# Extra full-size products on TensorE in the gate's chain and between the two merged matrices

## The chip, the cores and the metric

The kernel runs on one core of one Trainium2 chip. A core has five engines with queues of their own: TensorE (PE in the profile, its weight loads PEld), VectorE (DVE), ScalarE (ACT), GpSimd (POOL) and SyncE (SP), which issues DMAs. They run at the same time and wait for one another through semaphores. The metric is the time of one execution on the device, in microseconds. Lower is better.

## The reference

A small image-and-text transformer: 32 samples of 141 tokens (64 image patches and 77 text tokens), 128 wide. A tokenizer is followed by attention (one head), a feed-forward layer whose weights are merged for each sample, attention with eight heads, and a mixture of eight experts with two chosen for each token. The change lies in the merged feed-forward layer:

```
gh  = relu(x @ gfc1_w.T + gfc1_b)
g   = (gh @ gfc2_w.T + gfc2_b).mean(over the sample's tokens)   # 8 gate values for each sample
W1m = W1 + sum_e g[b,e] * tv_W1[e]                              # 512 x 128, one for each sample
b1m = b1 + g @ tv_b1
W2m = W2 + sum_e g[b,e] * tv_W2[e]                              # 128 x 512, one for each sample
h   = relu(x @ W1m.T + b1m)
out = h @ W2m.T + b2m
```

## The kernel before

Activations lie transposed, feature by partition: `hT` is the residual stream and `xn` the normalised one, both 128 x 4512, and each engine has its program written out by hand. `ln_pe` (L615, L621) makes a norm in twelve chunks of `CH` = 376 columns, with products of 128x128 by 128x376. PSUM is eight banks: `ps` is banks 0 and 1, `ps3a` banks 2 to 4, `ps3b` banks 5 to 7.

Around the change the work goes in four stages.

1. The gate's hidden layer: sixteen products of 282 columns (L954), ScalarE's relu (L1292), VectorE's sums over the tokens (L1527) into `ghm`.
2. The gate's chain, in which each step waits for the last: TensorE multiplies `ghm` by `gfc2` (L956), VectorE sets `g9` (L1531, L1533), TensorE spreads it over the partitions (L958), VectorE makes `gcol` and `gblk` (L1535, L1537). Between, TensorE makes the merged biases with five products of 32 columns (L961), which VectorE copies out (L1540).
3. The merge: the rows of both matrices come as products with `gblk`. Of each row of the matrices the base and its eight task vectors are nine inputs, three rows go into one product, so a product has 27 active rows and 96 columns (three rows by 32 samples). Four products stand in the array at once, in its four groups of 32 rows, and write four banks (L969). Twenty products are a set, with one load of 320 KB (`tvc`, five buffers deep, issued by SyncE at L499 when the set five before it is done). There are `SETS` = 18 sets, the last with four products only; `W1_SETS` = 9 of them make the first matrix. Sets alternate between banks 0 to 3 and banks 4 to 7; ScalarE copies two banks of a set into `arena` (L1298) and VectorE the other two (L1545). TensorE begins set s when set s-2 has been copied out.
4. The feed-forward layer: for each of 32 samples four products with the first matrix (L991), relu on ScalarE and VectorE (L1313, L1314, L1555), four products with the second (L1001). The merged weights of a sample are first gathered from `arena` into `wst`, the first matrix by ScalarE (L1308; for samples 0 and 1 by GpSimd, L687, as soon as nine sets are done), the second by GpSimd (L693). These loops wait for all 18 sets.

Of the kernel before, what the change touches and what calls it, by code (L numbers as in the profile page):

```python
# [33 lines left out]
CH = 376  # L34
# [33 lines left out]
W1_SETS = -(-F // (20 * NJ))  # L68
# [52 lines left out]
def reuse(eng, sem, u, depth):  # L121

    if is_known(u):
        if u >= depth:
            eng.wait_ge(sem, u - depth + 1)
    else:
        eng.wait_ge(sem, u - depth + 1)
# [84 lines left out]
def early_fusion(nc, patches, text, noise, vectors, turned, spread, tok, attn0, ffn, attn1, moe, mrows, const, out):  # L212
# [3 lines left out]
    with ExitStack() as ctx:  # L216
        def sb(name, shape, dt=F32, scope=None):
            return (scope or ctx).enter_context(nc.sbuf_tensor(name, shape, dt))
# [8 lines left out]
        def S(name):  # L227
            if name not in sems:
                sems[name] = ctx.enter_context(nc.semaphore(name))
            return sems[name]  # L230
# [5 lines left out]
        bank = [ps[0][:, :], ps[1][:, :]] + [ps3a[:, i, :] for i in range(3)] + [ps3b[:, i, :] for i in range(3)]  # L236

        hT = sb("hT", [P, T])
        xn = sb("xn", [P, T])
# [9 lines left out]
        def C(name, rows=P):  # L249
            a, n = CONST[name]  # L250
            return cst[0:rows, a:a + n]
# [4 lines left out]
        def W(name):  # L256
            return wT[:, SLOT[name], :]
# [145 lines left out]
        def chunk(buf, c, n=CH):  # L403
            return buf[:, bass.ds(c * n, n)]
# [21 lines left out]
        def normed(eng, name, chunks):  # L426

            eng.wait_ge(S("ln_out"), NCH * NORMS.index(name) + chunks)
# [236 lines left out]
        def _(pool):  # L665
# [97 lines left out]
            def scatter(g, i):  # L763
                src, _, rows = rows_of(g, i)
                if i == SPLIT[g] + g:
                    pool.wait_ge(S("xs_clear"), 16)
                    pool.wait_ge(S("x2_set"), SPLIT[g + 1] + g + 1)
                    pool.wait_ge(S("aux_set"), g + 1)
                for k, buf in enumerate((src, xr2[0:rows, i])):
                    pool.indirect_dma_start(xs[:, :], bass.IndirectOffsetOnAxis(ap=m_at[0:rows, k, i:i + 1], axis=0),  # L770
                                            buf, None, oob_is_err=True).then_inc(S("scattered"), 16)
# [39 lines left out]
        def _(pe):  # L811
# [138 lines left out]
            for t in range(B // 2):  # L950
                if t < 4:
                    normed(pe, "ln2", 9 + t)
                reuse(pe, S("gh_done"), t, 4)
                pe.matmul(bank[t % 4][:, 0:GB], W("gfc1"), chunk(xn, t, GB), start=True, stop=True).then_inc(S("gh_mm"), 1)  # L954
            pe.wait_ge(S("gh_sum"), B // 2)
            pe.matmul(bank[4][0:E, 0:B], W("gfc2")[:, 0:E], ghm[:, :], start=True, stop=True).then_inc(S("g_mm"), 1)  # L956
            pe.wait_ge(S("g9_ready"), 2)
            pe.matmul(bank[5][:, 0:B], C("rep", E + 1), g9[:, 0:B], start=True, stop=True).then_inc(S("grep_mm"), 1)  # L958
            pe.wait_ge(S("tvb_in"), 64)
            for k in range(5):  # L960
                mm = pe.matmul(bank[6][:, k * B:(k + 1) * B], tvb[:, k * P:(k + 1) * P], g9[:, 0:B], start=True, stop=True, skip_group_check=True)  # L961
            mm.then_inc(S("bm_mm"), 1)
            pe.wait_ge(S("gblk_ready"), 1)

            def merge(n, r, h):
                pe.wait_ge(S(f"tv_in{r}"), n * 16 + 16)
                for c in range(min(5, NM - 5 * (5 * n + r))):
                    for i in range(4):
                        mm = pe.matmul(bank[4 * h + i][:, c * NJ * B:(c + 1) * NJ * B], tvc[32 * i:32 * i + KM, r, c * P:(c + 1) * P],  # L969
                                       gblk[32 * i:32 * i + KM, :], start=True, stop=True, skip_group_check=True)  # L970
                mm.then_inc(S("mg_mm"), 1)
            for s in range(SETS):
                if s == 1:
                    pe.wait_ge(S("bm_copied"), 1)
                if s >= 2:
                    pe.wait_ge(S("mg_act"), s - 1)
                    pe.wait_ge(S("mg_dve"), s - 1)
                merge(s // 5, s % 5, s % 2)
            pe.wait_ge(S("mg_act"), SETS)
            pe.wait_ge(S("mg_dve"), SETS)  # L980
# [1075 lines left out]
```

## Time and profile before

| | us |
|---|---|
| runs shown (3) | 745.31, 745.4, 747.85; median 745.4 |
| profiled execution, its own time | 745.01 |
| its span | 743.2 |
| PE busy | 638.4 (86%) |
| DVE / ACT / POOL busy | 501.8 / 443.5 / 307.6 |
| granted TensorE clock, mean over the span | 0.911 |

The span is what the profiler records of the program; the execution's own time is 1.8 us more. The granted clock is a share of 2.4 GHz: 1.00 is 2.4 GHz and 0.50 is 1.2 GHz. In a timeline a row is a run of like instructions: start, length, engine, line, operation, tiles (out<-in), count, and in brackets the idle time before it with what ended it. "128x480 f32" is partitions by elements.

### The profile page before, as it was taken

Reading aid. Unit: us, or ns where it says so; the run is one execution under the profiler, and the core shown is the slowest. Engines: PE = TensorE matmul, PEld = TensorE weight load, DVE = VectorE, ACT = ScalarE, POOL = GpSimd, SP = SyncE. Lnnn points to the kernel's source line nnn. Section 1 sums busy time; section 2 is a strip of 40 time slices with the busy share of each in tenths; the row PEclk is TensorE's granted clock in tenths of the full one; section 3 lists DMA queues with packets and bytes.
Section 4 is the critical chain, followed back from the end, with each engine's and each line's share of the span. In section 5 each row is a group of like instructions: output and inputs, shape, how many; then the busy total and the mean of one; then the engine's idle time right before and its main releaser. Section 6 shows DMA issues by size and latency. Waiting matters only on the chain.

```text
span 743.2 us, 17507 instructions
## 1 busy us (share of the span) xinstructions
PE 638.4 (86%) x5635; PEld 541.0 (73%) x5635; DVE 501.8 (68%) x1399; ACT 443.5 (60%) x1185; POOL 307.6 (41%) x502
## 2 busy tenths in 40 slices
PE   5698999899999998999989988946889999999800
PEld 2247986699999656888878877835879888888700
DVE  4446784655455564888898895866787787878614
ACT  4386455744888697777767764603646566656500
POOL 0200000001555301222354686589772376777642
PEclk9999999955999998999999997977899999999955
DMA  8911323053000499940000000000142778888547
GB/s 257 280 52 65 120 96 105 1 144 90 1 0 0 164 353 360 334 136 2 2 3 2 31 27 20 23 32 19 48 128 58 250 274 273 283 276 282 188 145 265
DMA packets 65639, 96.39 MB, mean 130 GB/s; under 512 B 6279, under 2 KB 48868, under 8 KB 65573
## 3 DMA queue, kind: packets, MB, share of 16 engines
q1 hardware_dynamic: 56004, 82.64, 34.6%
q0 software_dynamic: 5344, 10.80, 4.1%
q10 hardware_dynamic: 4224, 2.10, 0.9%
q8 instruction: 38, 0.62, 0.3%
q14 instruction: 29, 0.23, 0.1%
HBM read 51.25 MB, written 44.26 MB: 129 GB/s over the span
## 4 chain that ended last, share of the span: by engine, by line
PE 46%; POOL 15%; DVE 12%; ACT 11%; issue 9%; DMA 5%; SPq 1%; POOLq 0%; DVEq 0%; ACTq 0%
POOL rows_by_token L800 9%; PE ps L1062 3%; DMA rows_by_token<-yrow,homei 3%; PE ps3b L1102 3%; POOL rows_by_expert L770 3%; PE ps L969 2%; PE ps L991 2%; PE ps3a L991 2%; PE ps3b L1001 2%; PE ps3a L1089 2%; PE ps3a L1001 2%; DVE h_f L1891 2%; ACT wst L646 2%; PE ps3b L969 1%; PE ps L817 1%
## 5 line engine op out<-in xcount | busy, mean ns | idle before, releaser
L800 POOL DMA_INDIRECT rows_by_token<-yrow,homei x93 | 94.4, 1015 | 57.6 <-DVE yrow L1909 30.9
L1395 ACT CAST h_hi<-h_f 128x384 fp32r<-128x384 f32 x86 | 44.1, 513 | 76.6 <-DVE h_f L1891 69.6
L1345 ACT ACTIVATE arena<-ps3a,arena 128x141 f32<-128x141 f32 x192 | 55.7, 389 | 7.8 <-DVE arena L1775 7.1
L1914 DVE TENSOR_TENSOR h_lo<-h_f,h_hi 128x384 fp32r<-128x384 f32 x86 | 47.8, 556 | 17.6 <-ACT h_hi L1395 16.7
L693 POOL COPY wst<-arena 128x512 f32 (+1 forms) x32 | 36.0, 1127 | 41.1 <-DVE arena L1545 15.3
L1751 DVE RECIPROCAL arena<-ps 128x141 f32<-128x141 f32 x32 | 33.3, 1042 | 23.0 <-PE ps L1065 23.0
L1327 ACT ACTIVATE arena<-ps,vec,cst 128x141 f32<-128x141 f32 x32 | 15.1, 471 | 48.8 <-PE ps L1080 47.9
L1775 DVE TENSOR_REDUCE arena<-ps3a 128x2 f32<-128x282 f32 x96 | 38.6, 443 | 6.4 <-PE ps3a L1089 6.3
L770 POOL DMA_INDIRECT rows_by_expert<-xr,m_at x36 | 35.7, 992 | 11.0 <-issue 11.0
L770 POOL DMA_INDIRECT rows_by_expert<-xn,m_at x32 | 34.2, 1070 | 8.3 <-issue 8.3
L969 PE MATMUL ps3a<-gblk,tvc 27*128 27x96 f32 x262 | 36.2, 413 | 0.0
L969 PEld LDWEIGHTS ps3a<-gblk,tvc 27*128 27x128 f32 x262 | 35.1, 311 | 0.0
L734 POOL COPY arena<-arena 128x104 f32<-128x104 f32 x32 | 8.7, 272 | 63.6 <-ACT arena L1347 63.6
L1102 PE MATMUL ps3b<-cst,arena 128*128 128x128 f32 x256 | 34.7, 280 | 0.0
L1308 ACT COPY wst<-arena 128x512 f32 (+1 forms) x30 | 34.2, 1140 | 0.0
L726 POOL TENSOR_TENSOR arena<-arena,cst 128x104 f32<-128x104 f32 x32 | 11.9, 372 | 50.4 <-ACT arena L1329 50.1
L1891 DVE TENSOR_TENSOR h_f<-ps,h_s 128x384 f32<-128x384 f32 x43 | 23.9, 556 | 12.8 <-ACT h_s L1392 6.4
L1102 PEld LDWEIGHTS ps3b<-cst,arena 128*128 128x128 f32 x256 | 30.6, 146 | 0.0
L687 POOL COPY wst<-arena 128x512 f32<-128x512 f32 x2 | 2.0, 1061 | 67.0 <-DVE arena L1545 67.0
L1124 PE MATMUL ps3a<-h_hi,wb 128*128 128x384 f32 x62 | 26.2, 423 | 4.0 <-issue 2.1
L682 POOL COPY arena<-xn 128x52 f32<-128x52 f32 x8 | 1.8, 232 | 61.5 <-PE ps3b L916 42.4
L1089 PE MATMUL ps3a<-arena 32*128 32x141 f32 x384 | 26.4, 310 | 0.1
(405 smaller groups left out, 2324.7 us busy)
## 6 DMA issues: line engine op xcount, KB each, us to landing
rows_by_expert<-zeros SPq DMA_DIRECT2D x1, 18915.0 KB, 61.1
wb<-expert_parts SPq DMA_DIRECT2D x31, 512.0 KB, 4.0
wb<-expert_parts SPq DMA_DIRECT2D x31, 256.0 KB
expert_parts<-arena SPq DMA_DIRECT2D x18, 384.0 KB, 2.8
xrow<-rows_by_expert SPq DMA_DIRECT2D x31, 195.0 KB
tvc<-merge_rows SPq DMA_DIRECT2D x18, 320.0 KB, 3.0
rows_by_token<-zeros SPq DMA_DIRECT2D x2, 2304.0 KB, 44.9
ysum<-rows_by_token SPq DMA_DIRECT2D x10, 320.0 KB, 6.0
```

What stands on the lines that cost most here:

```text
L693: pool.tensor_copy(wst[:, r, F:2 * F], merged_for(1, t)).then_inc(S("f_w2"), 1)
L770: pool.indirect_dma_start(xs[:, :], bass.IndirectOffsetOnAxis(ap=m_at[0:rows, k, i:i + 1], axis=0), buf, None, oob_is_err=True).then_inc(S ...
L800: pool.indirect_dma_start(yt[:, :], bass.IndirectOffsetOnAxis(ap=homei[:, q, s:s + 1], axis=0), yrow[:, q, s, :], None, oob_is_err=True).t ...
L969: mm = pe.matmul(bank[4 * h + i][:, c * NJ * B:(c + 1) * NJ * B], tvc[32 * i:32 * i + KM, r, c * P:(c + 1) * P], gblk[32 * i:32 * i + KM, ...
L1089: mm = pe.matmul(bank[2 + i][:, e * N:e * N + N], b_q[rows, q, e, 0:P], b_k[rows, q, :], start=True, stop=True, skip_group_check=True)
L1102: mm = pe.transpose(bank[6 + h // 4][:, (h % 4) * P:(h % 4) * P + P], b_e[:, r, h, 0:P], ident)
L1308: act.copy(wst[:, r, 0:F], merged_for(0, t)).then_inc(S("f_w1"), 1)
L1345: ins = act.activation(b_e[:, q, h, :], bank[2 + i][:, (h % 2) * N:(h % 2) * N + N], ACT.Exp, bias=b_nm[:, q, h:h + 1])
L1395: act.copy(h_hi[:, s, 0:n], h_f[:, s, 0:n]).then_inc(S("h_hi"), 1)
L1775: dve.tensor_reduce(b_nm[:, q, 2 * i:2 * i + n], bank[2 + i][:, 0:n * N].rearrange("p (h n) -> p h n", h=n), AX, ALU.max, negate=True).the ...
L1891: dve.tensor_tensor(h_f[:, s, :], bank[UB_[k]][:, 0:M], h_s[:, s, :], ALU.mult).then_inc(S("prod"), 1)
L1914: dve.tensor_tensor(h_lo[:, s, :], h_f[:, s, :], h_hi[:, s, :].bitcast(F32), ALU.subtract).then_inc(S("h_lo"), 1)
```

## The change

The change adds nine products of 128x128 by 128x376 that nothing reads, of the constant matrix `centre` with a chunk of `xn`. Two stand behind the gate's hidden layer, one behind the product with `gfc2`, and one behind the five bias products, all into bank 7 (`keep_running`). Five stand between set 8 and set 9 of the merge, behind set 9's waits, into bank 4, which set 9 then overwrites. No other instruction and no wait changes.

```
+            def keep_running(n):
+                pe.matmul(bank[7][:, 0:n], C("centre"), chunk(xn, 0, n), start=True, stop=True, skip_group_check=True)
+            for k in range(2):
+                keep_running(CH)
             pe.wait_ge(S("gh_sum"), B // 2)
             pe.matmul(bank[4][0:E, 0:B], W("gfc2")[:, 0:E], ghm[:, :], start=True, stop=True).then_inc(S("g_mm"), 1)
+            keep_running(CH)
             pe.wait_ge(S("g9_ready"), 2)
             pe.matmul(bank[5][:, 0:B], C("rep", E + 1), g9[:, 0:B], start=True, stop=True).then_inc(S("grep_mm"), 1)
             pe.wait_ge(S("tvb_in"), 64)
             for k in range(5):
                 mm = pe.matmul(bank[6][:, k * B:(k + 1) * B], tvb[:, k * P:(k + 1) * P], g9[:, 0:B], start=True, stop=True, skip_group_check=True)
             mm.then_inc(S("bm_mm"), 1)
+            keep_running(CH)
             pe.wait_ge(S("gblk_ready"), 1)
...
                 if s >= 2:
                     pe.wait_ge(S("mg_act"), s - 1)
                     pe.wait_ge(S("mg_dve"), s - 1)
+                if s == W1_SETS:
+                    for k in range(5):
+                        pe.matmul(bank[4 * (s % 2)][:, 0:CH], C("centre"), chunk(xn, k, CH), start=True, stop=True, skip_group_check=True)
                 merge(s // 5, s % 5, s % 2)
```

TensorE's row in the program between the gate's hidden layer and the first set, before (`ghm`, `g` and `gblk` are the gate's tiles, `tvb` the bias rows, `tvc` a set's load):

```order
L954 MATMUL ps3a<-xn,wT 128x282 x2
L956 MATMUL ps3a<-ghm,wT 8x32
L958 MATMUL ps3b<-g,cst 128x32
L961 MATMUL ps3b<-g,tvb 128x32 x5
L969 MATMUL ps<-gblk,tvc 128x96 x2
```

The same place in the changed kernel:

```order
L954 MATMUL ps3a<-xn,wT 128x282 x2
L957 MATMUL ps3b<-xn,cst 128x376 x2
L961 MATMUL ps3a<-ghm,wT 8x32
L957 MATMUL ps3b<-xn,cst 128x376
L964 MATMUL ps3b<-g,cst 128x32
L967 MATMUL ps3b<-g,tvb 128x32 x5
L957 MATMUL ps3b<-xn,cst 128x376
L976 MATMUL ps<-gblk,tvc 128x96 x2
```

The four new products are the rows of L957; the fourth stands between the bias products and set 0.

TensorE's row where set 8 (banks 0 to 3) ends and set 9 (banks 4 to 7) begins, before:

```order
L969 MATMUL ps<-gblk,tvc 128x96 x2
L969 MATMUL ps3a<-gblk,tvc 128x96 x3
L969 MATMUL ps3b<-gblk,tvc 128x96 x3
L969 MATMUL ps3a<-gblk,tvc 128x96
L969 MATMUL ps3b<-gblk,tvc 128x96 x3
```

And in the changed kernel:

```order
L976 MATMUL ps<-gblk,tvc 128x96 x2
L976 MATMUL ps3a<-gblk,tvc 128x96 x2
L987 MATMUL ps3a<-xn,cst 128x376 x5
L976 MATMUL ps3a<-gblk,tvc 128x96
L976 MATMUL ps3b<-gblk,tvc 128x96 x3
L976 MATMUL ps3a<-gblk,tvc 128x96
```

The three products "ps3a x3" of before were the last two of set 8 and the first of set 9; the five new ones now stand between them.

## Rows read from the trace of the kernel before

**Rows 1.** The page: busy time, and TensorE's granted clock in 40 slices of 18.6 us.
```profile
PE 638.4 (86%) x5635; PEld 541.0 (73%) x5635; DVE 501.8 (68%) x1399; ACT 443.5 (60%) x1185; POOL 307.6 (41%) x502
PEclk9999999955999998999999997977899999999955
```

**Rows 2.** Stretch, length; busy and count of PE, PEld, DVE, ACT, POOL; PEclk; DMA.
```profile
140.50:143.90 3.40, 3.38 (x15) 2.35 (x13) 3.19 (x8) 3.40 (x8) 0.00 (x0) 1.00 0.00 0
143.90:147.30 3.40, 1.81 (x28) 1.68 (x29) 1.73 (x8) 0.51 (x2) 0.00 (x0) 1.00 0.00 0
147.40:183.40 36.00, 36.00 (x681) 36.00 (x675) 19.89 (x33) 16.32 (x32) 2.05 (x2) 0.50 0.43 121
183.40:185.10 1.70, 0.45 (x6) 0.21 (x1) 1.55 (x4) 1.31 (x4) 0.00 (x0) 0.50 0.00 0
185.10:188.20 3.10, 3.04 (x13) 3.07 (x14) 0.63 (x2) 0.70 (x3) 2.05 (x2) 0.50 0.00 0
```

**Rows 3.** Timeline of PE, from the gate's hidden layer to the first sets.
```profile
142.77 1.11 PE L954 MATMUL ps3a<-xn,wT 128*128 128x282 f32 x4
144.95 0.23 PE L956 MATMUL ps3a<-ghm,wT 128*8 128x32 f32 x2 [1.07 <-DVE ghm L1527]
145.72 0.40 PE L958 MATMUL ps3b<-g,cst 9*128 9x32 f32 x2 [0.55 <-DVE g L1533]
...
146.87 0.35 PE L969 MATMUL ps3a<-gblk,tvc 27*128 27x96 f32 x2
...
147.06 0.28 PE L969 MATMUL ps3a<-gblk,tvc 27*128 27x96 f32 x2
...
147.17 0.28 PE L969 MATMUL ps3a<-gblk,tvc 27*128 27x96 f32 x2
```

**Rows 4.** Timeline of PE where set 1 ends and set 2 begins, and of DVE.
```profile
150.91 0.42 PE L969 MATMUL ps<-gblk,tvc 27*128 27x96 f32 x1
...
151.13 0.42 PE L969 MATMUL ps<-gblk,tvc 27*128 27x96 f32 x1
...
151.51 1.22 DVE L1545 COPY arena<-ps3b 128x480 f32<-128x480 f32 x2 [0.81 <-PE ps3b L969]
153.64 1.22 DVE L1545 COPY arena<-ps3a 128x480 f32<-128x480 f32 x2 [0.91 <-PE ps3a L969]
```

**Rows 5.** Timeline of PE in the norm before the gate.
```profile
124.83 0.80 PE L621 MATMUL ps3b<-wst,cst 128*128 128x376 f32 x2
125.47 0.80 PE L615 MATMUL ps<-hT,cst 128*128 128x376 f32 x2
```

**Rows 6.** DMA issues of 140 to 200 us, and the rate in 40 slices of 1.5 us.
```profile
GB/s 0 0 0 0 0 0 11 217 97 154 199 167 90 179 213 71 180 208 123 141 178 212 65 184 205 13 0 0 0 0 0 0 0 11 0 0 0 0 0 0
tvc<-merge_rows SPq DMA_DIRECT2D x13, 320.0 KB, 3.0
```

**Rows 7.** Timeline where the feed-forward layer begins.
```profile
185.16 2.22 PE L991 MATMUL ps<-xn,wst 128*128 128x141 f32 x8 [1.31 <-ACT arena L1298]
185.19 2.05 POOL L693 COPY wst<-arena 128x512 f32<-128x512 f32 x2 [15.35 <-DVE arena L1545]
...
188.69 1.13 PE L1001 MATMUL ps3a<-hbuf,wst 128*128 128x141 f32 x8
...
189.65 1.12 PE L991 MATMUL ps<-xn,wst 128*128 128x141 f32 x8
189.85 0.37 DVE L1560 SCALAR_TENSOR_TENSOR xn<-ps3a,bmb,xn 128x141 f32<-128x141 f32 x1 [0.33 <-PE ps3a L1001]
```

**Rows 8.** Busy time of stretches elsewhere, columns as in rows 2.
```profile
399.90:403.30 3.40, 2.06 (x26) 1.64 (x25) 3.30 (x14) 1.64 (x6) 0.96 (x4) 1.00 0.00 0
...
287.30:290.60 3.30, 2.94 (x23) 2.26 (x22) 1.97 (x6) 3.30 (x14) 1.09 (x4) 1.00 1.06 361
```

**Rows 9.** TensorE's products by line in 399.9 to 403.3, then in 287.3 to 290.6.
```profile
L1089 PE MATMUL ps3a<-arena 32*128 32x141 f32 x12 | 0.8, 304 | 0.0
...
L1089 PE MATMUL ps3a<-arena 32*128 32x141 f32 x12 | 2.0, 319 | 0.1
```

More of the change, by code:

```diff
@@ L954, in _, with keep_running @@
                 pe.matmul(bank[t % 4][:, 0:GB], W("gfc1"), chunk(xn, t, GB), start=True, stop=True).then_inc(S("gh_mm"), 1)
+            def keep_running(n):
+                pe.matmul(bank[7][:, 0:n], C("centre"), chunk(xn, 0, n), start=True, stop=True, skip_group_check=True)
+            for k in range(2):
+                keep_running(CH)
             pe.wait_ge(S("gh_sum"), B // 2)
             pe.matmul(bank[4][0:E, 0:B], W("gfc2")[:, 0:E], ghm[:, :], start=True, stop=True).then_inc(S("g_mm"), 1)
+            keep_running(CH)
             pe.wait_ge(S("g9_ready"), 2)
@@ L962, in _ @@
             mm.then_inc(S("bm_mm"), 1)
+            keep_running(CH)
             pe.wait_ge(S("gblk_ready"), 1)
@@ L977, in _ @@
                     pe.wait_ge(S("mg_dve"), s - 1)
+                if s == W1_SETS:
+                    for k in range(5):
+                        pe.matmul(bank[4 * (s % 2)][:, 0:CH], C("centre"), chunk(xn, k, CH), start=True, stop=True, skip_group_check=True)
                 merge(s // 5, s % 5, s % 2)
```

## The prediction
> **What bounds the kernel now.** I read the page first: TensorE is busy for 86% of the span, and the strip of its granted clock, which is 9 nearly everywhere, has two slices of 5 at 149 to 186 us, the ninth and tenth of the strip [rows 1]. So the next view was busy time by stretch around there [rows 2]. The reader is to see three things. In the gate's chain, 143.9 to 147.3 us, TensorE was busy for 1.81 of 3.40 us, with thin products, and still had clock 1.00. In the merge, 147.4 to 183.4, it was busy for 36.00 of 36.00 us at 0.50, which is 1.2 GHz, while VectorE worked 19.89 and ScalarE 16.32 us: TensorE alone bounds this stage, at half its speed. The clock came back only after 3 us of full-size feed-forward products (185.1 to 188.2).
>
> Then the timelines, for what a set of the merge costs. Groups of four L969 products follow one another every 0.11 us before the clock fell (146.87, 147.06, 147.17, the first pair with a bias product between) [rows 3] and every 0.22 us after (150.91, 151.13) [rows 4]. A set of 20 products is ten such steps: 2.13 us, as VectorE's copies of it are apart (151.51, 153.64), and 1.07 us at clock 1.00. VectorE's two copies of a set take 1.22 us, and it waited 0.91 us before each.
>
> **The change part by part.** A product of 376 columns takes 0.63 us in a stream at clock 1.00 (124.83, 125.47) [rows 5]; at 0.50 no row shows one, and I estimate twice that, 1.26 us, as the merge's steps double.
>
> First and second new product. The gate layer's last four records start at 142.77 and stream 0.24 us each (0.63 x 282/376 / 2), to 143.71; two products more end at 144.97. The product with `gfc2` started at 144.95, after 1.07 us of waiting for VectorE's sums [rows 3]. Cost 0 to 0.05 us; the cover is that wait.
>
> Third: from about 145.05 to 145.68, where TensorE waited for `g9` until 145.72 [rows 3]. Cost 0 to 0.05 us.
>
> Fourth: it stands behind the bias products, and the merge followed on them with no gap (146.87 and 147.06 are sets' products already). Nothing hides it: 0.65 us. What is queued behind it is set 0, for which ScalarE and VectorE wait. For all four I take +0.7 us; bounds 0.6 and 1.0.
>
> What they buy, if it comes: the low-work stretch at clock 1.00 after which the clock fell now holds 1.9 to 2.5 us of full-size products in 3.4 us, against none. I expect the clock to stay at 1.00 there. No row shows this chain with them.
>
> The merge at clock 1.00. TensorE then needs 1.07 us for a set, less than VectorE's 1.22, so what is late next is the handing back of banks. Set s+2 starts when set s has been copied out: product time 1.07, from the set's end to VectorE's first copy 0.38, copies 1.22, back to TensorE 0.08. The 0.38 is an estimate: at half clock it was 0.60 (150.91 to 151.51) [rows 4], and in the feed-forward layer at clock 1.00 VectorE began 0.20 us after the set of products ended (189.65 to 189.85) [rows 7]; it lies between. A cycle of two sets is 2.75 us, a set 1.38. From set 0's start, set 9 would start at 4 x 2.75 + 1.25 = 12.25 us.
>
> The five products before set 9. They stand behind its waits, so they begin when it could have begun: +3.13 us (5 x 0.63) for set 9 and all odd sets behind it; VectorE copies set 8 in the meantime and then waits. Set 17 starts at 26.4 and set 16 at 24.9; set 16 is copied out at 27.6, set 17 (a fifth of a set) 0.4 us later, and the feed-forward layer starts at 28.1. Before, it was 185.16 - 146.86 = 38.3 [rows 3, 7]. Gain 10.2 us.
>
> Bounds on the set's time. Below: VectorE alone, 1.22 us, which gives another 2.6 us. Above: the loads. 13 of the 18 sets' loads go during the merge, 320 KB each; the highest rate of a slice was 217 GB/s [rows 6], which is 1.51 us for a set and costs 13 x 0.13 = 1.7 us. They land in 3.0 us [rows 6] and are issued four sets, 5.5 us, ahead, so I take them as hidden. If a load of every set were late by all that the clock gains, the gain would be 0.
>
> The feed-forward start. L991's first start to L1001's first took 3.53 us at clock 0.50; in the steady part such a pair of steps is 1.92 (two of 188.69 to 189.65) [rows 7]. GpSimd's first copy of two (2.05 us from the start) ends within it. Gain 1.6 us; bounds 0 and 1.8. It is 0 where the clock falls at the merge's end, where TensorE has about 1.5 us without work and a short set before it, as now (0.45 busy of 1.70 us) [rows 2]: I give that 4 in 10, at 1.6 us.
>
> GpSimd's copies of the first matrix for samples 0 and 1 move earlier with set 8; nothing waits for them. All that follows is a chain without a fixed time in it, so it moves as a whole. But the later falls of the clock (slices of 7 and 8) [rows 1] need not repeat as they were: one of them, shown as an 8 in an 18.6 us slice, is worth some 2 us either way.
>
> Sum: +0.7 - 10.2 - 1.6 = -11.1 us against the profiled execution's 745.0, so 733.9; the median of the runs is 0.4 above that execution, so 734.3. With part of the risk at the merge's end, 734.5.
>
> One rule of the Trainium skill ("TensorE: Matmul & The Clock Gate", LDWEIGHTS) speaks against this sum: it gives a weight load as its columns over 1.2, in ns, at whatever clock, and a set is bound by its loads. By it a set would take 2.13 us still. The steps of 0.11 us at clock 1.00 [rows 3] are against it. The same page (What's actually happening) says that activity releases the throttle; with TensorE busy for all of 36.00 us at 0.50 [rows 2] the trace does not agree for 27-row products, and if it did the change would have nothing to win beyond the first microseconds.
>
> **The rivals.** The question is whether the merge, which did not raise the clock in 36 us, holds it. For: it stayed at 1.00 in stretches with fewer products and real gaps, as at 399.9 to 403.3 (busy 2.06 of 3.40 us, with 32-row products among them). Against: it fell after 287.3 to 290.6, where TensorE was busy for 2.94 of 3.30 us, most of it with 32-row products [rows 8, 9]. Raising and holding need not ask the same of the engine, and the merge at full rate leaves gaps of only a fifth.
>
> A. It falls in both halves (the slower side). Per us at clock 1.00 the merge gains (2.13 - 1.38) / 1.38 = 0.55 us. Against it stand 0.7 us and the five products, which at half clock until it rises (about 3.1 us, as at the feed-forward start) cost 3.1 + 2.5 x 0.63 = 4.7 us. So the change loses if the merge has less than 10 us at clock 1.00 in all. With 2 us in each half: 745.4 + 5.4 - 2.2 = 748.6; with none 750.8.
>
> B. It falls in the first half only, after some 3 us, and the five products bring it back for good: 0.7 + 4.7 - 1.7 (3 x 0.55) - 8 sets x 0.75 - 1.6 = -3.9, 741.5.
>
> C. The loads bound the sets at up to 1.51 us: 736.
>
> D. A set is no faster at clock 1.00: 0.7 + 3.13 - 1.6 = +2.2, 747.6. Only the rule of the skill speaks for it; the measured steps against.
>
> **How the numbers follow.** Forecast 0.66; A 0.14; B 0.13; C 0.04; D 0.03. The forecast's own range is 730.5 to 738: below by VectorE's bound and a later fall that is gone, above by the fall at the feed-forward start and a later one more. With C and most of B the range is 730 to 743. A measurement of this kernel tells about 0.5%, 3.7 us. Faster than 741.7: 0.66 + 0.04 + 0.6 of B = 0.78. Within: the rest of B, D, and the part of A with some full clock, 0.17. Slower: 0.05.
>
> **What would show it.** Clock 1.00 from 144 us on through the merge; VectorE's pairs of copies 1.3 to 1.4 us apart, with one hole of about 3 us more before set 9's; set 0 some 0.7 us after its old time; the first L991 at about 175.6 and the first L1001 1.9 us behind it; the span about 11 us shorter and the stages behind 190 us unchanged. I am wrong if the clock is 0.50 in the merge (A, B), if pairs are over 1.5 us apart with TensorE waiting for `tvc` (C), or if the steps of L969 stay at 0.21 us at clock 1.00 (D).

## The result and the profile after

The changed kernel takes 732.97 us (median of four, 732.7 to 733.94) against 746.09 before (745.31 to 747.85): ratio 0.9846, 95% interval 0.9815 to 0.9878. Timed again on another chip it was 733.3 against 743.14, ratio 0.9878 (0.9832 to 0.9924). The forecast was 734.5 in a range of 730 to 743. The ratios leave out executions that lie more than 1.5% above the fastest of their kernel, and they are not the quotients of the medians beside them.

Single executions of one kernel lie several us apart (before: 735.5 to 749.5 in one group of eleven), and their mean clock differs with them (0.926 in the first, 0.909 in the last). In the two profiles of the changed kernel, and of the kernel with three products (e3, e6), the clock's falls stand at different places. So below the profiles are compared stage by stage, and totals only as medians.

Busy time by stretch of the changed kernel, columns as in [rows 2]: the chain, sets 0 to 8, the five products, sets 9 to 16, the end of the merge, the feed-forward start.

```profile
143.90:147.30 3.40, 3.40 (x20) 2.23 (x19) 1.42 (x7) 0.01 (x1) 0.00 (x0) 1.00 0.00 0
147.70:159.80 12.10, 10.97 (x350) 10.30 (x352) 9.23 (x16) 8.16 (x16) 0.00 (x0) 1.00 0.63 177
159.90:163.00 3.10, 3.10 (x25) 2.00 (x21) 1.30 (x3) 1.02 (x2) 1.27 (x2) 1.00 0.81 253
163.00:173.20 10.20, 9.42 (x290) 8.48 (x290) 7.06 (x12) 6.12 (x12) 0.80 (x1) 1.00 0.47 138
...
174.80:178.00 3.20, 2.22 (x19) 2.08 (x19) 1.45 (x5) 1.22 (x6) 1.89 (x2) 0.82 0.00 0
```

The chain has no empty stretch left, and the clock is 1.00 through the merge, where before it was 0.50 from 0.5 us behind its start on. It falls just behind the merge, in the first feed-forward products (0.82 over 174.8 to 178).

The timeline of TensorE through the chain, which answers to [rows 3]. L957 is the new line, L976 the merge.

```profile
142.26 1.11 PE L954 MATMUL ps3a<-xn,wT 128*128 128x282 f32 x4
143.21 1.42 PE L957 MATMUL ps3b<-xn,cst 128*128 128x376 f32 x4
144.57 0.22 PE L961 MATMUL ps3a<-ghm,wT 128*8 128x32 f32 x2
144.72 0.90 PE L957 MATMUL ps3b<-xn,cst 128*128 128x376 f32 x2
145.55 0.40 PE L964 MATMUL ps3b<-g,cst 9*128 9x32 f32 x2
145.80 1.28 PE L967 MATMUL ps3b<-g,tvb 9*128 9x32 f32 x10
147.00 0.90 PE L957 MATMUL ps3b<-xn,cst 128*128 128x376 f32 x2
147.83 0.35 PE L976 MATMUL ps<-gblk,tvc 27*128 27x96 f32 x2
```

The last gate products started 0.51 us earlier in this execution than in that of before, so set 0, at 147.83 against 146.86, is 1.48 us late. The first two products cost 0.13 us (L961 at 144.57 against 144.95 less 0.51), the third 0.21 more (L964), and the fourth the rest, 1.1.

The copies by VectorE, which answer to [rows 4]:

```profile
157.62 1.22 DVE L1555 COPY arena<-ps3a 128x480 f32<-128x480 f32 x2 [0.40 <-PE ps3a L976]
158.76 1.21 DVE L1555 COPY arena<-ps3b 128x480 f32<-128x480 f32 x2
160.37 1.22 DVE L1555 COPY arena<-ps3a 128x480 f32<-128x480 f32 x2 [0.40 <-PE ps3a L976]
165.04 1.22 DVE L1555 COPY arena<-ps3b 128x480 f32<-128x480 f32 x2 [3.44 <-PE ps3b L976]
166.18 1.21 DVE L1555 COPY arena<-ps3a 128x480 f32<-128x480 f32 x2
```

The copies of every second set are 2.75 us apart (157.62, 160.37), where it was 2 x 2.13. Set 9's come at 165.04 in place of 161.51 (158.76 + 2.75): the five products cost 3.53 us at that place. Set 10's follow on them at once, at 166.18, in place of 163.12 (160.37 + 2.75), so the even sets behind the five are 3.06 us late and not 3.53.

The start of the feed-forward layer, which answers to [rows 7]. L1001 is L991 of before, L1011 is L1001.

```profile
174.81 0.28 PE L976 MATMUL ps3b<-gblk,tvc 27*128 27x96 f32 x3
176.08 1.51 PE L1001 MATMUL ps<-xn,wst 128*128 128x141 f32 x8 [0.98 <-ACT arena L1308]
177.38 2.09 PE L1001 MATMUL ps3a<-xn,wst 128*128 128x141 f32 x8
179.26 1.61 PE L1011 MATMUL ps3a<-hbuf,wst 128*128 128x141 f32 x8
```

TensorE had no work for about 1 us after the short last set, the clock fell some way into the first products, and L1011 starts 3.18 us behind L1001 (3.53 before, 1.92 forecast without a fall).

By stage, in us, the profiled executions of all kernels. "Chain" is from the gate layer's first product (L954) to the merge's first, "merge" from there to the first feed-forward product, "start" from there to the first product with the second matrix, "sum" from the gate layer's first product to the last of the feed-forward layer.

| kernel | chain | merge | start | sum | fall in the merge |
|---|---|---|---|---|---|
| before | 11.71 | 38.30 | 3.52 | 113.44 | at its start |
| changed | 13.18 | 28.24 | 3.18 | 105.00 | no (at its end) |
| changed, again | 13.19 | 28.39 | 2.12 | 103.68 | no |
| e1: four, no five | 13.19 | 26.34 | 2.12 | 101.63 | no |
| e2: five only | 11.75 | 37.62 | 3.59 | 112.87 | at its start, back at the five |
| e3: first three | 12.05 | 25.88 | 2.12 | 100.03 | no |
| e4: four of 32 rows | 12.19 | 39.12 | 3.89 | 115.62 | at its start |
| e6: first three, again | 12.05 | 25.63 | 2.12 | 99.78 | no |
| e7: three and one at the end | 12.05 | 26.01 | 2.12 | 100.16 | no |
| e8: first two | 11.83 | 38.02 | 3.80 | 113.57 | at its start |
| e9: third only | 12.20 | 38.71 | 3.89 | 115.30 | at its start |
| e10: four, short fourth | 12.77 | 31.07 | 3.89 | 108.33 | half way |
| e11: three and one before set 9 | 12.05 | 25.91 | 2.12 | 100.06 | no |
| e12: three and two before set 9 | 12.05 | 27.34 | 3.57 | 102.97 | no (at its end) |

Only the changed kernel and the kernel with three products were profiled twice; each other row is one execution.

Of the 11.1 us by which the changed kernel's profiled span is shorter, 8.4 lie in these stages, 0.5 ahead of them and 2.1 to 2.2 behind, where the clock's falls came at other places. The strip of the clock after has no 5 at 149 to 186 us any more, against [rows 1]:

```profile
PEclk9999999999999997999999999976899999999955
```

### The profile page after: what moved, and what is told of

It is laid out like the page before. It is cut to its first block, busy times and chain, and to the rows that moved or that the text cites. A ratio compares the mean times of both kernels' runs of the same rounds, so it can differ in the third digit from the quotient of the medians.

```text
span 732.1 us, 17543 instructions
## 1 busy us (share of the span) xinstructions
PE 624.2 (85%) x5653; PEld 524.9 (72%) x5653; DVE 503.4 (69%) x1399; ACT 443.7 (61%) x1185; POOL 304.8 (42%) x502
## 4 chain that ended last, share of the span: by engine, by line
PE 61%; DVE 11%; ACT 10%; POOL 7%; issue 5%; DMA 4%; SPq 1%; POOLq 0%; DVEq 0%; ACTq 0%
PE ps3a L1134 4%; PE ps L1072 3%; PE ps3b L1112 3%; PE ps3a L1136 3%; PE ps3a L1135 3%; POOL rows_by_expert L770 3%; PE ps3a L1099 2%; PE ps3a L1001 2%; PE ps L1001 2%; PE ps3a L1011 2%; PE ps3b L1011 2%; DMA wb<-expert_parts 2%; PE ps L1134 2%; PE ps L1136 2%; PE ps L1135 2%
## 5 line engine op out<-in xcount | busy, mean ns | idle before, releaser
L743 POOL TENSOR_SCALAR xn<-hT,m_mv,m_rs 128x128 f32<-128x128 f32 x32 | 25.8, 805 | 0.3 <-ACT m_rs L1371 0.2
L1099 PE MATMUL ps3b<-arena 32*128 32x141 f32 x128 | 24.9, 315 | 0.0
```

Source lines behind the costliest of these rows:

```text
L1099: mm = pe.matmul(bank[2 + i][:, e * N:e * N + N], b_q[rows, q, e, 0:P], b_k[rows, q, :], start=True, stop=True, skip_group_check=True)
```

## The experiments

All are the changed kernel with an edit. "Held" means clock 1.00 through the merge.

**e1, the chain's four products without the five.**

```
-                if s == W1_SETS:
-                    for k in range(5):
-                        pe.matmul(bank[4 * (s % 2)][:, 0:CH], C("centre"), chunk(xn, k, CH), ...)
```

> The four products of the chain without the five before set 9. Theory 1 (the chain's products keep the clock at 1.00 and the merge holds it; the five are a cost): set 9's copies come 3.5 us earlier than in the changed kernel, clock 1.00 through the merge, 733.0 - 3.5 = 729.5 us. Theory 2 (the five are needed to hold the clock in the second half): it falls in the second matrix's sets, which then take 2.13 instead of 1.38 us; about 3 us slower than the changed kernel, 736.

Median 735.05 us (728.84 to 739.59, four runs) against 742.59 before; ratio 0.9889 (0.9801 to 0.9978). In the profile the merge held, in both halves:

```profile
147.90:160.20 12.30, 11.17 (x362) 10.63 (x364) 9.40 (x16) 8.16 (x16) 0.00 (x0) 1.00 0.64 183
160.30:174.20 13.90, 11.60 (x332) 10.47 (x327) 11.14 (x20) 9.47 (x20) 2.07 (x2) 1.00 0.51 150
```

So the five are not what holds it in that execution. But the merge is only 1.9 to 2.1 us shorter than in the two profiles of the changed kernel, not 3.5, and the median is no lower than the changed kernel's 733 (with 733.0 - 3.5 = 729.5 expected). Two things are in the merge's part of this. The five had cost the even sets 3.06 us and not 3.5. And in set 10 VectorE waited 1.53 us where it had waited 0.40, and TensorE stood still ahead of it with nobody to wait for:

```profile
161.57 1.21 DVE L1552 COPY arena<-ps3b 128x480 f32<-128x480 f32 x2
164.32 1.22 DVE L1552 COPY arena<-ps3a 128x480 f32<-128x480 f32 x2 [1.53 <-PE ps3a L976]
```
```profile
162.48 0.42 PE L976 MATMUL ps<-gblk,tvc 27*128 27x96 f32 x4
163.60 0.35 PE L976 MATMUL ps3a<-gblk,tvc 27*128 27x96 f32 x2 [0.70 <-issue]
```

This is a stop of 0.70 us with the releaser "issue", within set 10. The changed kernel's merge has no such stop of the matmuls; whether the five covered it isn't shown, since e3 and e6 below have no five either and no long stop. One run of the four had a mean clock of 0.93 and 739.59 us; e10 shows one fall that may stand behind that, if not the only one.

**e2, the five without the chain's four.**

```
-            for k in range(2):
-                keep_running(CH)
...
-            keep_running(CH)      # the third
...
-            keep_running(CH)      # the fourth
```

> The five products before set 9 without the four of the chain. Theory 1: the clock falls in the chain as before, nine sets go at 2.13 us, the five start at 1.2 GHz and bring the clock back, costing about 4.7 us; eight sets then gain 0.75 us each and the start of the feed-forward layer up to 1.6: 746.1 + 4.7 - 6.0 - 1.6 = 743 us, 745 if the clock falls again at the merge's end. Theory 2 (the five give most of the gain): 736 or less.

Ratio 0.9961 (0.9913 to 1.0008); median 742.03 against 742.59, ten runs from 732.01 to 748.94. The stretches, sets 0 to 8, the five, sets 9 to 17, feed-forward start:

```profile
147.40:167.30 19.90, 19.90 (x352) 19.44 (x349) 10.77 (x19) 9.03 (x18) 0.00 (x0) 0.50 0.48 135
167.40:170.80 3.40, 3.40 (x7) 1.76 (x7) 0.26 (x1) 0.05 (x1) 2.02 (x2) 0.58 0.35 96
170.90:183.80 12.90, 11.15 (x331) 9.91 (x329) 9.57 (x18) 8.45 (x18) 0.00 (x0) 1.00 0.36 105
184.10:187.60 3.50, 3.50 (x16) 3.50 (x17) 0.64 (x2) 1.20 (x3) 2.02 (x2) 0.54 0.00 0
```

Theory 1 holds in the totals and in this profile: the chain's products make the gain. The clock rose while the five ran, and the second half then kept it, but they began at 166.28 and set 9 at 171.59, 5.31 us, which eats most of what the eight sets gain; the clock fell again at the end. One run, 732.01 us with a mean clock of 0.942, is as fast as the changed kernel; it has no profile, so whether its merge held is open.

**e3, the first three products of the chain.** The fourth and the five are out.

```
             mm.then_inc(S("bm_mm"), 1)
-            keep_running(CH)
```

> Only the first three products of the chain: the fourth, behind the bias products, and the five are out. Theory 1: the first three stand in waits that TensorE has anyway and are enough; the fourth cost 1.1 us of its own. Clock 1.00 through the merge, 729.5 - 1.1 = 728.4 us. Theory 3 (the bias products and the merge's first set have too little work in them without the fourth): the clock falls at the merge's start, 746 us or a little more.

Median 729.93 us (725.48 to 734.41), ratio 0.9806 (0.9737 to 0.9876). The merge held, and set 0 came 1.14 us earlier than with four (12.05 against 13.19).

```profile
150.10:175.90 25.80, 22.23 (x692) 20.82 (x691) 20.81 (x37) 17.64 (x36) 2.09 (x2) 1.00 0.58 169
```

The fourth isn't needed, and theory 3 falls for three products. The profiled run is the slowest (734.41 us, mean clock 0.935); it had falls of the clock at 57 and 64 us, far ahead of the change, so a low mean clock alone doesn't tell that the merge fell.

TensorE stood still for less at the place of e1's stop, with no product before set 9:

```profile
165.01 0.27 PE L975 MATMUL ps3a<-gblk,tvc 27*128 27x96 f32 x1
165.43 0.24 PE L975 MATMUL ps3a<-gblk,tvc 27*128 27x96 f32 x1
```

From start to start that is 0.42 us in place of a step of 0.11; in e1 it was 0.97, and in the second profile of this kernel (e6) no such gap stands there. The merge is 0.5 to 0.7 us shorter than e1's (25.88 and 25.63 against 26.34).

**e4, four products with 32 active rows.** Their length is the same, but a quarter of the array's rows is used.

```
-                pe.matmul(bank[7][:, 0:n], C("centre"), chunk(xn, 0, n), ...)
+                pe.matmul(bank[7][:, 0:n], C("centre")[96:P, :], chunk(xn, 0, n)[96:P, :], ...)
```

> As the first kernel of these (four products in the chain, no five), but the four have 32 active rows of 128, the same 128 output rows and 376 columns and so the same length. Theory 1 (full-size work holds the clock; thin products, as the merge's, count for little): the clock falls at the merge's start as before, and the products are only a cost, 746.1 + 1.5 = 747.6 us. Theory 4 (any products that fill the gaps hold it): clock 1.00 in the merge, 729.5 us.

Median 743.83 against 742.59, ratio 1.0021 (0.9985 to 1.0057). The chain was as full of products as ever (first row), and the clock fell all the same:

```profile
141.00:145.90 4.90, 4.90 (x26) 3.11 (x24) 3.44 (x10) 2.33 (x5) 0.00 (x0) 1.00 0.00 0
146.30:183.70 37.40, 37.40 (x693) 37.40 (x691) 19.99 (x33) 16.31 (x32) 2.07 (x2) 0.50 0.41 117
```

Theory 4 falls. Filling the gaps doesn't do it: products of 128 rows did, those of 32 didn't (nothing between was tried). The total is 3.8 us under the 747.6 that was expected, of which 3.5 is that the kernel before ran at 742.59 here and not at 746.1; against it e4 is 1.2 us slower, where 1.5 was expected. The chain is only 0.5 us longer than before (12.19), so thin products between thin ones delay less than full-size ones; the rest of the 2.2 us by which its sum is longer comes behind, where the clock was down already at the first set (from 145.9 us on).

**The changed kernel again (e5), three products again (e6), three and one at the merge's end (e7), two products (e8)**, in one group on one chip.

> The changed kernel once more, on the chip and beside the kernels of this group, since single runs of one kernel spread over some us. Theory 1: from the gate layer's first product to the feed-forward layer's last 105.0 us, or 103.4 where the clock does not fall at the merge's end; 8.4 to 10 less than before; total 9 to 13 us below before.

> The first three products of the chain alone, again, beside the changed kernel. Theory 1: 3 to 5 us less than the changed kernel of this group (the five cost 3.5 in place, the fourth 1.1), 100 us from the gate layer's first product to the feed-forward layer's last. Rival: the total is the same within 1 us because the falls of the clock behind the merge come back and even it out.

> The first three products, and one more between set 16 and set 17 of the merge, where TensorE waits for the copies anyway. Theory 5 (the clock falls at the start of the feed-forward layer in part of the runs, for lack of work at the merge's end, at some 1.7 us): 0.5 us less than the three alone on average and no run with a fall there; the product itself costs at most 0.3 us. Rival: no fall there without it either, so it only costs, up to 0.3 us.

> Only the first two products of the chain. Behind them stand the product with gfc2, 0.5 us of waiting, the spreading product and the bias products, all thin. Theory 1: two full-size products in the stretch after which the clock fell are enough in most runs, 100 us from gate layer to feed-forward end; total as with three. Theory 3: the 2 us of thin work and waiting behind them let it fall at the merge's start, 113 us and the total of before.

```
# e7: three products, and in the loop over the sets
+                if s == SETS - 1:
+                    pe.matmul(bank[4][:, 0:CH], C("centre"), chunk(xn, 0, CH), ...)
# e8: as e3, without the third product as well
```

| | median | runs | ratio to before (743.14) |
|---|---|---|---|
| e5, changed | 733.3 | 728.89 to 734.57 | 0.9878 (0.9832 to 0.9924) |
| e6, three | 728.9 | 727.67 to 734.81 | 0.9846 (0.9794 to 0.9898) |
| e7, three and end | 732.41 | 731.09 to 738.49 | 0.9883 (0.9831 to 0.9935) |
| e8, two | 734.36 | 728.55 to 738.01 | 0.9869 (0.9805 to 0.9933) |

The changed kernel's stages (e5) took 103.68 us here, near the 103.4 of theory 1 without a fall at the end. In place, three products are 3.9 us shorter than four and the five (99.78 against 103.68); the medians say 4.4, but the intervals of the ratios overlap. In e6 four runs lie at 727.67 to 729.01 with a mean clock of 0.946 and more, and two at 733.51 and 734.81 with 0.936 and less.

e7 isn't settled. Its profile has no fall at the feed-forward start and nor has that of e6; the medians don't show a gain, and in place the extra product costs at most 0.4 us (100.16 against 99.78, and 100.03 in e3).

e8 suggests that two are on the edge. In the profiled run the chain had full-size work only at its start (first row), and the clock fell for the whole merge; another run, 728.55 us with a mean clock of 0.947, is like those of kernels whose merge held; it wasn't profiled.

```profile
142.40:145.70 3.30, 2.75 (x36) 2.09 (x38) 1.53 (x7) 0.06 (x1) 0.00 (x0) 1.00 0.00 0
146.00:181.30 35.30, 35.30 (x668) 35.30 (x665) 19.55 (x32) 16.32 (x32) 2.05 (x2) 0.50 0.44 123
```

**e9, the third product alone, and e10, four with a fourth of 128 columns, no five.**

```
# e9
-            for k in range(2):
-                keep_running(CH)
# e10: as e1, and behind the bias products
-            keep_running(CH)
+            keep_running(P)
```

> Only the third product of the chain, in the wait for g9. Theory 1 by amount: one full-size product in the chain is less than the two that held only in part of the runs, so the clock falls at the merge's start in most; 113 us from gate layer to feed-forward end, total as before. Theory 1 by place: what counts is that no wait stays without full-size work; the one product breaks up the chain and holds the clock, 100 us.

> The four products of the chain, no five, with the fourth of 128 columns in place of 376. The fourth at full length put set 0 of the merge 1.14 us later than with three products (13.19 against 12.05 us from the gate layer's first product to set 0), where its streaming is 0.63 us. If the rest is a fixed cost of a full-size product between thin ones, 0.21 us of streaming and 0.5 fixed: 12.75 us. If the cost goes with the length, 12.05 + 1.14 x 128/376 = 12.44 us.

e9: 744.03 against 743.03, ratio 1.0051 (1.001 to 1.0093); the clock was 0.50 from 146.3 us on, 115.30 us in place. One product in the middle is only a cost, so it isn't enough to break up the wait: the amount counts. With e8 and e3: one didn't hold it, with two it fell in the profile and may have held in part of the runs, three held it in both profiles. Whether the place counts as well isn't shown, since three products at another place weren't tried.

e10 is a single run: 737.31 us against 743.03. The chain took 12.77 us where 12.75 was expected for a fixed cost. That is 0.72 more than with three products, of which 0.21 is the streaming of 128 columns; some 0.5 doesn't depend on the length. A reading of it, which wasn't tried by itself, is that a full-size product separates the thin ones on its two sides: before, the merge's first products began while bias products were still running,

```profile
146.86 0.34 PE L969 MATMUL ps<-gblk,tvc 27*128 27x96 f32 x1
146.97 0.27 PE L961 MATMUL ps3b<-g,tvb 9*128 9x32 f32 x1
```

and in the changed kernel the fourth stands between the two.

Its profile had one thing that no other showed:

```profile
151.00:163.00 12.00, 10.87 (x361) 10.33 (x360) 9.40 (x16) 8.16 (x16) 0.00 (x0) 1.00 0.66 189
163.10:166.40 3.30, 2.43 (x73) 2.12 (x72) 2.35 (x4) 2.04 (x4) 1.91 (x2) 1.00 0.84 236
166.60:180.00 13.40, 13.40 (x255) 13.40 (x251) 7.33 (x12) 6.12 (x12) 0.00 (x0) 0.50 0.30 92
```
```profile
166.21 0.35 PE L976 MATMUL ps3a<-gblk,tvc 27*128 27x96 f32 x2 [0.62 <-issue]
```

The merge ran at 1.00 for 16 us, then came the stop in set 10, and behind it the clock was 0.50 to the merge's end: 31.07 us in place of 26. So the fall of theory 2 came in one execution without the five. That the stop brought it on is a guess from the order in time, and that the five would have prevented it isn't shown. Nor can it be said of the other runs with 0.93 to 0.936: this run had 0.936, and e3's profiled run, whose merge held, had 0.935.

**e11 and e12, three products and one or two before set 9.** Is one product before set 9 enough against the stop and the fall?

```
# as e3, and in the loop over the sets
+                if s == W1_SETS:
+                    for k in range(1):      # e12: range(2)
+                        pe.matmul(bank[4 * (s % 2)][:, 0:CH], C("centre"), chunk(xn, k, CH), ...)
```

> The first three products of the chain, and one product before set 9 in place of five. Where the five were out, TensorE stood still for 0.7 us or so around set 11 without any engine to wait for, and in one run the clock fell behind that for the rest of the merge. Theory 6 (a product there covers this stop and keeps the clock in all runs; one is enough): set 9's copies at most 1.1 us late, no later stop, 100 us from gate layer to feed-forward end, total 4 us below the changed kernel, 729 us, and no run with a mean clock under 0.94. Rival (the stop stays where it is whatever stands before set 9): the stop comes on top of the product, 101 us, and single runs still fall.

> As the kernel with one product before set 9, with two. Theory 6: 0.6 us more than with one, 100.6 us from gate layer to feed-forward end, no stop around set 11, total 729.5 us, the clock held in all runs. Rival: as with one, plus 0.6 us.

e11: median 731.53 (728.61 to 732.65), ratio 0.9845 (0.979 to 0.99). e12: 729.99 (725.39 to 733.08), ratio 0.9838 (0.9781 to 0.9896); before 744.5. Neither has a long stop; the longest with the releaser "issue" was 0.2 us:

```profile
PE ps L975 <- issue: 0.2, 1, 0.2
```

That isn't the product's doing as far as is shown: e6, with three products and none before set 9, has no long stop either, and e11's sum of 100.06 us is that of e3 and e6 (100.03 and 99.78). The long stop was seen only with four products in the chain and no five (e1, e10). The twelve runs are within 725.39 and 733.08 us, and one has a mean clock of 0.938, the others 0.941 and more, where without any product there single runs went to 734.81 (e6) and 739.59 (e1); these were other groups on other chips, so that the spread is smaller is not shown. Theory 6 had said that no run would be under 0.94, and that e12 would take 100.6 us. Beside e11, e12 lost 2.9 us: a fall at the merge's end (1.45 at the start) and 1.4 in the merge, more than twice the streaming of its one more product.

The ratios of e3, e6, e11 and e12 are all under 0.9878, that of the changed kernel when timed again, and only e3's interval, which ends at 0.9876, leaves it out; so which of them is best isn't settled. That they beat the changed kernel rests on the stages of single profiles: 3.6 to 3.9 us against its better one for e3, e6 and e11, and 0.7 for e12.

## Why the prediction was right

The forecast's sum was -11.1 us, and the profiled execution came out 11.1 us shorter (733.94 against 745.01). The agreement to the tenth is luck: the three terms came to -8.9 us in place of -11.1, and the rest of the program, where the change does nothing, gave the other 2.2.

**The clock held.** Forecast at 0.66. It held in eight of the nine profiles with three or more full-size products in the chain; in the ninth, e10, it fell half way. e4 shows that it is the full-size work, not the filling, and e2 that without it the merge starts at half clock. What I gave as the reason, full-size work in the stretch ahead of the merge, is what e4, e8 and e9 bear out. Rivals A and B didn't come about, though B's second half is what e2 is made of: I expected the five to cost 4.7 us there and they cost 5.3.

**Products one to four: +0.7 forecast, +1.5 measured.** The first three were nearly hidden (0.34 us, against 0 to 0.1). The fourth was mis-sized: 1.14 us, not 0.65. I counted its streaming and not the 0.5 us that it costs whatever its length (e10). The sum lies beyond my bound of 1.0 for all four.

**The merge: -10.2 forecast, -10.06 measured.** The two-set cycle of 2.75 us was right, with its 0.38 us from a set's end to the copies; 28.24 us from set 0 to the feed-forward layer, where 28.1 was forecast. So the copies and the handing back of banks bound it, and rival C is out: the loads landed in a median of 3.6 us, under the 5.5 of their lead, the rate of a slice went up to 291 GB/s (I had taken 217 as the bound), and TensorE's waits in the merge name the copies and not `tvc`. They name ScalarE's, but VectorE's pair ends later: ahead of set 17, which began at 174.62, ScalarE's ended at 174.32 and VectorE's at 174.52.

By steps of 0.11 us at clock 1.00, rival D is out too. I had read the rule of the Trainium skill ("TensorE: Matmul & The Clock Gate", LDWEIGHTS) wrongly: columns over 1.2 are 107 ns for the 128 columns of these loads, and a set is ten steps, so an estimate from the page is 1.07 us for a set and not 2.13. With that the trace agrees at clock 1.00. At 0.50 it does not: the steps were 0.21 to 0.22 us, and a record of a load took 328 ns in place of 187. So nothing spoke for D.

**The five: 3.13 forecast, 3.53 measured** at set 9, some 0.4 us beyond their streaming. Taking them out brings less than 3.5 in the merge: 1.9 to 2.1 us in e1, and 2.4 to 2.8 in e3 and e6. At most 3.06 could come back for the even sets. What is missing from that is in e1 the stop in set 10 (VectorE waited 1.13 us more there), which no row of before showed and no step of mine had; in e3 and e6 it is 0.3 to 0.7 us, of which the hold of 0.42 us in e3 is a part.

**The feed-forward start: -1.6 forecast, -0.3 measured in one profile, -1.4 in the other.** The fall at the merge's end was given 4 in 10; it came in the first profile and not in the second.

**The rest.** I gave the later falls some 2 us either way; what lies behind the stages gave 2.1 to 2.2 in the first profile.

## What to carry to other kernels

Where TensorE's clock falls after a chain of small dependent steps, and the work behind it is too thin to raise the clock, unread full-size products in the waits of that chain can be worth far more than they cost: here 1.9 us of them cost 0.34 us and kept the 26 us of the merge at double speed, in both profiles of that kernel. Put them only where the engine waits anyway, count a fixed cost of some 0.5 us beside their length where they separate thin products, and find the least number that holds by profiles of several executions.

## What the runs showed that was not expected

- Products of 32 rows in the chain, with TensorE busy 4.90 of 4.90 us, did not keep the clock at 1.00, and the merge's 27-row products, which never raised it in 36 us, did keep it (e1, e3). So thin work that did not raise the clock could still hold it, if not in every execution (e10). The Trainium skill ("TensorE: Matmul & The Clock Gate", What's actually happening) tells of how busy the engine has been; a full busy share was not enough here.
- A stop of 0.62 to 0.70 us in TensorE with the releaser "issue", in set 10, in e1 and e10, which the merge at half clock didn't have. Counted in TensorE's matmul records from the program's start it stands behind the same one, the 1208th, in both, and so does the hold of 0.42 us in e3, although e3 has a product less in its chain. In e1 one block of instructions (0.02 MB) was transferred between 160.0 and 163.5 us, around it (the stop ended at 163.60), at 2.6% of the time of 16 DMA engines, which is 1.46 us, while the loads were busy at 77.6%:

```profile
q1 hardware_dynamic: 358, 0.81, 77.6%
q8 instruction: 1, 0.02, 2.6%
```

  The Trainium skill ("Runtime: NRT & Kernel Launch", Instruction fetch mechanics) tells of instructions fetched in 16 KiB blocks, mostly hidden behind the issue of those before. That the stop is such a block coming late is a guess that fits, with the fixed place in the stream too; it wasn't tried.
- Ten of the changed kernel's runs have a mean clock of 0.941 to 0.946, and before's total ranged over 14 us (735.46 to 749.48) in one group, whose mean clocks went from 0.926 to 0.909.
